# A masked attention block with residual norms: turned x kept twice by parity instead of copied, V's part of TensorE's loop written twice, and other ring sizes

## The reference

```python
qkv = (x @ w_qkv).reshape(b, n, 3, H, hd).transpose(2, 0, 3, 1, 4)
q, k, v = (qkv[0], qkv[1], qkv[2])
attn = jnp.einsum('bhnd,bhmd->bhnm', q, k) * scale
attn = jnp.where(attn_mask[None, None] == 0, -jnp.inf, attn)
attn = jax.nn.softmax(attn, axis=-1)
o = jnp.einsum('bhnm,bhmd->bhnd', attn, v).transpose(0, 2, 1, 3).reshape(b, n, d)
o = o @ w_proj + b_proj
...
return o + ln          # ln: layer norm of o with gamma and beta
...
x = _layernorm(x + _L0_gnn_ref(x, ...), axis=-1)
```

## Time and profile before

| | us |
|---|---|
| median of 3 runs | 3217.51 |
| lowest to highest | 3217.07 to 3221.09 |
| the profiled execution | 3214.41 |
| its span in the trace | 3212.6 |
| TensorE busy in it | 3035.8 |
| VectorE busy | 2481.6 |
| ScalarE busy | 2621.1 |
| GpSimd busy | 2500.2 |

### The profile page before, as it was taken

The page is one execution under the profiler, slowest core; times in us unless marked ns, Lnnn a source line. Parts: engine busy times, 40 slices in busy tenths (PEclk is TensorE's granted clock), DMA queues, the critical chain, the costliest instruction groups (busy, mean ns, idle before and its releaser), DMA issues.

```text
span 3212.6 us, 121377 instructions
## 1 busy us (share of the span) xinstructions
PE 3035.8 (94%) x42504; PEld 1892.9 (59%) x42504; DVE 2481.6 (77%) x4601; ACT 2621.1 (82%) x3849; POOL 2500.2 (78%) x1543
## 2 busy tenths in 40 slices
PE   6989999999999999999999999999999999999984
PEld 3656656656665656656566666656656566665552
DVE  5567777878778787787878878787787877878775
ACT  5888888888888888888888888888888888888871
POOL 2777878787887878888787887878878788887883
PEclk9999999999999999999999999999999999999997
DMA  7999999999999999999999999999999999999993
GB/s 208 192 190 199 208 198 211 199 211 205 206 212 197 214 202 206 213 199 211 200 210 205 207 211 197 215 201 206 214 199 208 199 210 206 207 212 187 202 197 97
DMA packets 2187078, 648.05 MB, mean 202 GB/s; under 512 B 2135408, under 2 KB 2135408, under 8 KB 2186992
## 3 DMA queue, kind: packets, MB, share of 16 engines
q1 hardware_dynamic: 2133808, 548.28, 93.1%
q10 hardware_dynamic: 53184, 98.59, 9.3%
HBM read 76.28 MB, written 33.55 MB: 34 GB/s over the span
## 4 chain that ended last, share of the span: by engine, by line
POOL 45%; issue 31%; PE 10%; SPq 7%; DMA 2%; DVE 2%; ACT 1%; POOLq 1%; DVEq 0%; ACTq 0%
POOL p_split L780 37%; SPq L309 7%; POOL x_res L796 4%; PE scores_a L411 3%; PE side L375 2%; DMA pt<-p_split 2%; POOL norm L804 2%; POOL norm L799 2%; PE side L357 2%; PE proj L392 1%; PE pv_bank L432 1%; PE pv_bank L434 1%; PE pv_bank L433 1%; POOL shift L807 1%; POOLq L779 1%
## 5 line engine op out<-in xcount | busy, mean ns | idle before, releaser
L780 POOL TENSOR_TENSOR p_split<-p,p_split 128x1024 f16<-128x1024 f32 x1024 | 2178.6, 2144 | 642.8 <-ACT p_split L517 641.1
L504 ACT ACTIVATE p<-p,row_min 128x1024 f32<-128x1024 f32 x1024 | 1170.7, 1144 | 279.0 <-DVE row_min L662 277.1
L517 ACT ACTIVATE p_split<-p 128x1024 f16<-128x1024 f32 x1024 | 1047.2, 1046 | 120.4 <-DMA pt<-p_split 119.9
L432 PE MATMUL pv_bank<-v_both,pt 128*128 128x64 f16 x8192 | 830.5, 193 | 39.2 <-DMA pt<-p_split 31.2
L662 DVE CUSTOM_DVE_ANT_0 p<-scores_a,mask_q 128x1024 f32<-128x1024 f32 x512 | 626.2, 1223 | 309.4 <-PE scores_b L411 259.9
L434 PE MATMUL pv_bank<-v_both,pt 128*128 128x64 f16 x8192 | 831.4, 194 | 0.0
L433 PE MATMUL pv_bank<-v_both,pt 128*128 128x64 f16 x8192 | 831.3, 194 | 0.0
L432 PEld LDWEIGHTS pv_bank<-v_both,pt 128*128 128x128 f16 x8192 | 741.0, 98 | 126.5 <-issue 62.1
L433 PEld LDWEIGHTS pv_bank<-v_both,pt 128*128 128x128 f16 x8192 | 730.6, 98 | 67.9 <-issue 1.6
L434 PEld LDWEIGHTS pv_bank<-v_both,pt 128*128 128x128 f16 x8192 | 731.4, 98 | 0.0
L375 PE MATMUL side<-xt,w_hi 128*128 128x512 f16 x2048 | 636.0, 382 | 7.8 <-DVE q_lo L641 7.2
(11 more groups left out here) (80 smaller groups left out, 4411.2 us busy)
## 6 DMA issues: line engine op xcount, KB each, us to landing
x_in<-in_x ACTq DMA_DIRECT2D x60, 512.0 KB, 5.3
x_res<-in_x ACTq DMA_DIRECT2D x120, 256.0 KB, 3.5
out<-x_res ACTq DMA_DIRECT2D x120, 256.0 KB, 3.3
pt<-p_split SPq DMA_TRANSPOSE x1024, 4.9
pt<-in_adj SPq DMA_DIRECT2D x8, 512.0 KB, 10.0
ot<-in_L_gnn_w_qkv SPq DMA_DIRECT2D x4, 768.0 KB, 9.7
p<-in_x SPq DMA_DIRECT2D x8, 256.0 KB, 5.0
p<-in_x ACTq DMA_DIRECT2D x8, 256.0 KB, 8.5
```

Source lines behind the costliest of these rows:

```text
L432: nc.tensor.matmul(o, hi, v_hi, start=(kt == 0 and at == 0), stop=False, skip_group_check=True)
L504: nc.scalar.activation(p32[:, slot, :], p32[:, slot, :], ACT.Exp, bias=row_min[:, slot:slot + 1], scale=-1.0, accum_out=row_sum[:, head:he ...
L517: nc.scalar.activation(p_split[:, head % RING, HI, :], p32[:, head % RING, :], ACT.Copy).then_inc(hi_done, 1)
L780: nc.gpsimd.tensor_tensor(p_split[:, slot, LO, :], p32[:, slot, :], p_split[:, slot, HI, :], ALU.subtract).then_inc(lo_done, 1)
```

## The change

- `xt` becomes two whole sets of 8 tiles, by the parity of the batch. X writes into the other set; there are no copies, no Ifs on VectorE and no waits for copies on TensorE. TensorE's wait for X1 moves from K1 to Q0.
- Q and K now have both operands at a register's address. For V, whose weights must stand at a fixed address, TensorE's loop body has slots 4 to 11 twice, each in an If on the parity of the batch. With it the scores, the products with V and the first projection matmul that lie in these slots stand twice. Outside the loop nothing is doubled.
- `p_split` becomes a ring of 8 heads, `pt` one of 4: ScalarE waits for the transpose eight heads back, SyncE for the product with V four heads back.
- Slots: `COST` of Q 8 to 9 and of X 8 to 5, the first projection run 3 to 4 matmuls, VectorE's takes of V0, V1, X1 from 12, 12, 18 to 10, 11, 15, the load of x from 20 to 18, one norm step from 36 to 34. VectorE's takes wait without the separate no-op.

```diff
-TURNED = 8
+TURNED = 4
+SPLIT = 8
...
-ORDER = [("Q1", 0, 12), ("X0", 0, 4), ("V0", 0, 48), ("V1", 0, 48), ("P0", 0, 3), ("O1", 0, 4), ("P0", 3, 7),
+ORDER = [("Q1", 0, 12), ("X0", 0, 4), ("V0", 0, 48), ("V1", 0, 48), ("P0", 0, 4), ("O1", 0, 4), ("P0", 4, 7),
...
-COST = {"Q": 8, "V": 2.5, "O": 4, "K": 10, "P": 9, "X": 8}
+COST = {"Q": 9, "V": 2.5, "O": 4, "K": 10, "P": 9, "X": 5}
...
+V_SLOTS = [s for s in range(SLOTS) if any(kind[0] == "V" for kind, i in ITEMS[s])]
...
-TAKE_DVE = {"Q1": 4, "X0": 5, "V0": 12, "V1": 12, "O1": 14, "X1": 18, "Q0": 22, "K0": 29, "K1": 30, "O0": 30}
-
-COPY = [12, 13, 13, 15, 16, 17, 17]
-LOAD_X = 20
+TAKE_DVE = {"Q1": 4, "X0": 5, "V0": 10, "V1": 11, "O1": 14, "X1": 15, "Q0": 22, "K0": 29, "K1": 30, "O0": 30}
+LOAD_X = 18
...
-              {"stats": 30, "aggr": 31, "eps": 33, "add": 34, "power": 35, "scale": 36, "sum": 38, "stats2": 38,
+              {"stats": 30, "aggr": 31, "eps": 33, "add": 34, "power": 35, "scale": 34, "sum": 38, "stats2": 38,
...
-        xt = sb("xt", [P, 2 * T - 1, 2, KC, P], F16)
+        xt = sb("xt", [P, 2, T, 2, KC, P], F16)
...
-        p_split = sb("p_split", [P, RING, 2, N], F16)
+        p_split = sb("p_split", [P, SPLIT, 2, N], F16)
...
-                    mm = nc.tensor.matmul(bank[:, c * P:(c + 1) * P], xt[:, place(t), rows, k, :],
+                    mm = nc.tensor.matmul(bank[:, c * P:(c + 1) * P], xt[:, side_of_x, t, rows, k, :],
                                           w[:, k, OF_V, pair(g), :],
...
-                    if i == 0 and kind == "K1" and active(g, "X1"):
+                    if i == 0 and kind == NEXT_FIRST and active(g, "X1"):
                         wait_alone(pe, side_dve, side_done(g, "X1"))
-                    if i == 0 and kind == NEXT_FIRST:
-                        wait_alone(pe, x_copied[0], batch(g + 1))
-                    if i == 0 and kind == "K1":
-                        wait_alone(pe, x_copied[1], batch(g + 1))
...
-                                          xt[:, place(4 * half):place(4 * half) + 4, x_half, k, :],
+                                          xt[:, parity(batch(of)), 4 * half:4 * half + 4, x_half, k, :],
...
+            def stretch(g, slots, side_of_x):
+                for s in slots:
+                    u, j = s // QUARTERS, s % QUARTERS
+                    if j == 0 and active(g, "A"):
+                        unit_scores(g, u)
+                    if j % 2:
+                        times_v(g, u, j // 2)
+                    for kind, i in ITEMS[s]:
+                        side_matmul(g, kind, i, side_of_x)
+
             def body(g):
...
+                if known(g):
+                    stretch(g, range(SLOTS), parity(batch(g)))
+                    return
+                stretch(g, range(0, V_SLOTS[0]), None)
+                for side_of_x in range(2):
+                    with pe.If((batch(g) & 1) == side_of_x):
+                        stretch(g, range(V_SLOTS[0], V_SLOTS[-1] + 1), side_of_x)
+                stretch(g, range(V_SLOTS[-1] + 1, SLOTS), None)
...
-                before = unit_before(ug, uk, RING // 2)
+                before = unit_before(ug, uk, SPLIT // 2)
...
-                wait_alone(dve, side_act, side_done(g, kind))
+                wait(dve, side_act, side_done(g, kind))
...
-            def copy_tile(g, t):
-
-                if t == 0:
-                    wait_alone(dve, side_ready, side_done(g, "V1"))
-                    wait_alone(dve, side_dve, side_done(g, "X0"))
-                move = nc.vector.tensor_copy(xt[:, place(t), :, :, :].rearrange("p h k n -> p (h k n)"),
-                                             xt[:, waiting(t // 2, t % 2), :, :, :].rearrange("p h k n -> p (h k n)"))
-                if t in (3, 6):
-                    move.then_inc(x_copied[t // 4], 1)
```

More of the change, by code:

```diff
@@ L236, in bodies @@
                 body(g)
[L238 to L251, removed]
         def heads(g, u, ab):
@@ L333, in first_turn, with side_matmul @@
                 mm.then_inc(x_first_turned, 1)
-            def side_matmul(g, kind, i):
+            def side_matmul(g, kind, i, side_of_x):
                 if not active(g, kind):
@@ L470, in first_high @@
                 act.wait_ge(x_first_turned, t + 1)
-                nc.scalar.activation(xt[:, place(t), HI, :, :], side[t % 2][:, :].rearrange("p (k n) -> p k n", k=KC), ACT.Copy
+                nc.scalar.activation(xt[:, 0, t, HI, :, :], side[t % 2][:, :].rearrange("p (k n) -> p k n", k=KC), ACT.Copy
                                      ).then_inc(x_first_hi, 1)
@@ L489, in take @@
                 elif kind[0] == "X":
-                    nc.scalar.activation(xt[:, waiting(g, half), HI, :, :],
+                    nc.scalar.activation(xt[:, parity(batch(g + PAIRS)), pair(g) * 2 + half, HI, :, :],
                                          bank[:, :].rearrange("p (k n) -> p k n", k=KC), ACT.Copy).then_inc(side_act, 1)
@@ L512, in high_part @@
                 head = 2 * uk + ab
-                before = unit_before(ug, uk, RING // 2)
+                before = unit_before(ug, uk, SPLIT // 2)
                 if not known(before[0]) or before[0] >= 0:
-                    wait(act, turned[(head - RING) % TURNED], turned_before(before[0], before[1], ab) + 16)
+                    wait(act, turned[(head - SPLIT) % TURNED], turned_before(before[0], before[1], ab) + 16)
                 act.wait_ge(exp_done, heads(ug, uk, ab) + 1)
-                nc.scalar.activation(p_split[:, head % RING, HI, :], p32[:, head % RING, :], ACT.Copy).then_inc(hi_done, 1)
+                nc.scalar.activation(p_split[:, head % SPLIT, HI, :], p32[:, head % RING, :], ACT.Copy).then_inc(hi_done, 1)
             def last_norm(g, i):
@@ L630, in take @@
                 elif kind[0] == "X":
-                    tile = waiting(g, half)
-                    nc.vector.tensor_tensor(xt[:, tile, LO, :, :], bank[:, :].rearrange("p (k n) -> p k n", k=KC),
-                                            xt[:, tile, HI, :, :], ALU.subtract).then_inc(side_dve, 1)
+                    at, tile = parity(batch(g + PAIRS)), pair(g) * 2 + half
+                    nc.vector.tensor_tensor(xt[:, at, tile, LO, :, :], bank[:, :].rearrange("p (k n) -> p k n", k=KC),
+                                            xt[:, at, tile, HI, :, :], ALU.subtract).then_inc(side_dve, 1)
                 elif kind[0] == "V":
@@ L743, in body @@
                                 take(bg, kind)
-                    for t in range(7):
-                        if COPY[t] == s:
-                            at_end(dve, g, lambda: copy_tile(g, t))
                     for i in range(2):
```

21 lines of the change are left out of this document (6 added, 15 removed).

## The result

The kernel after takes 3854.5 us (median of 4 runs, 3851.4 to 3861.3), the kernel before on the same chip 3217.3 (3216.5 to 3221.1): a ratio of 1.198, 95% interval 1.196 to 1.200. The forecast was 3447 with a range up to 3570, so the sign was right and the size was not: 637 us slower, where 230 were forecast.

What follows compares the result with a forecast made beforehand. TensorE was taken to bound three passes in four, VectorE's copies adding 4.9 us to the fourth. Sum: 3214.4 - 74 + 11 + 292 = 3443.4, as a median of runs 3447 us; range 3140 to 3570.

Steps and rivals of the forecast that it cites:

- two stalls a pass: TensorE's loop: the branch back and one If wait for absent blocks, 2.7 us each, +292 us; 42%.
- The rival of a loop that stays: TensorE's loop: no block is fetched inside it, so 3155 us, from 3135 to 3200; 35%.
- that of one stall: TensorE's loop: only the branch back waits, the Ifs land on present blocks; +146, 3301 us (3240 to 3350); 17%.
- The count behind it: TensorE's program: 1957 instructions a pass, 7.6 blocks, touch nine, ten with the one in advance; eight were seen to stay.
- straight running hides a fetch: TensorE's loop: a block reached without a branch arrives without a stall; only branches to a non-next block wait.
- some 5 where the clock falls with it: TensorE's instruction fetch: upper bound of a stall, some 5 us instead of 3.5, if the clock falls too.
- bound of 4.4 us for a stall: TensorE's two waiting branches a pass: the most a stall costs, 475 us in all over 54 passes.
- Copies gone: Batch ends: 15 passes lose 4.9 us each without VectorE's tile copies, -74 us.
- Registers, Ifs, slots and takes: TensorE's loop: two Ifs a pass +11 us (0 to 45); Q and K register addresses 0; slots and takes 0.
- they run ahead of matmuls of 512 columns: TensorE's Q and K: added register instructions are hidden by running ahead; taken 0, at most 55 us.
- Rings: Split ring of eight, turned ring of four: 0 us, transposes having 4 us to spare; binding rival 3187 alone, 2%.
- a stall up to 3.8 us: Upper end of the predicted range: two stalls a pass, each up to this size, giving 3570 us.

Runs made afterwards that it cites:

- 1960 instructions: The kernel after with only its TensorE loop's first instruction laid on the start of a block: 3799.5 us, 1.181 to the kernel before.
- the unaligned loop: The kernel after with only V's own matmuls twice, in six pieces (1789 instructions), the loop starting in mid-block: 3692.2 us, 1.148 to the kernel before.
- the hinted one: The kernel after with a prefetch hint for the branch back's target at the top of each TensorE pass: 3624.5 us, 1.126 to the kernel before.
- the whole loop without copies: The kernel before without the seven tile copies and their waits, later batches reading the first batch's x: 3137.4 us, 0.9755 to the kernel before.
- the old rings: The kernel after with the ring sizes of before (four split heads, eight turned): 3831.6 us, 1.191 to the kernel before.
- V by register: The kernel after with slots 4 to 11 once, V's weights also at a register's address (1545 instructions): 3252.5 us, 1.012 to the kernel before.
- V alone, aligned: The kernel after with only V's matmuls twice, in six pieces (1789 instructions), loop start on a block's start: 3255.3 us, 1.012 to the kernel before.
- the second stretch alone: The kernel before with only TensorE's slots 4 to 11 written twice in two Ifs, both with the same addresses: 3879.3 us, 1.207 to the kernel before.

## Why the prediction was wrong, by its own steps

**The case was the right one.** Of the prediction's cases, two stalls a pass (42%) came true: ten blocks a pass, two waiting branches, at the branch back and at an If. The rival of a loop that stays (35%, 3155) and that of one stall (17%, 3301) fell by the ten fetches and the two branches of the first profile. The count behind it, from packets and passes alone, held to the block in the loops of 1789 and 1960 instructions. Its "straight running hides a fetch" held in the kernel after, but not in the unaligned loop nor in the hinted one. The one-stall rival rested on a block replaced only by the one eight further on; the unaligned one of the pair has all nine fetched instead, which excludes it.

**The step that failed is "two stalls a pass, each 2.7 us"**, +292. It took the packet's 1.1 us, a load's 2.2 and a lead of 0.6. Measured are branches of 4.6 and 5.0 us. The packet's own time was right (0.9 to 1.1 us as a rule); the round about it was not: from the branch's start to the packet's 1.4 to 3.2 us, with a median of 2.3 at the branch back, and from the packet's end to the next instruction some 1.4. A load's time to land was the wrong row to be nearest to, since nothing says that a fetch is issued as promptly, or that the engine goes on when it lands. TensorE's waits in the kernel after, over the loop alone, have the two stalls in their first row:

```profile
PE scores_a L389 <- issue: 476.1, 106, 5.5
PE pv_bank L410 <- DMA pt<-p_split: 26.8, 48, 0.9
PE side L353 <- issue: 15.4, 26, 0.6
```

**That is 4.5 us a stall, 9.0 a pass and 476 us, where 2.7, 5.4 and 292 were forecast.**

**The clock was left out of the sum**, the second part of the same step. The upper bound had it ("some 5 where the clock falls with it"), as an end of the range and not a term. The two rows below are the whole loop without copies and in the kernel after:

```profile
326.10:2815.40 2489.30, 2470.69 (x35199) 1549.96 (x35196) 1940.55 (x3711) 2161.57 (x3185) 2063.70 (x1273) 1.00 1.06 212
```

```profile
326.80:3532.90 3206.10, 2679.38 (x35194) 1622.78 (x35191) 1946.94 (x3711) 2179.78 (x3180) 2057.64 (x1273) 0.92 0.99 167
```

For the same matmuls TensorE is busy **3.9 us a pass longer, 209 us in all**. The clock can account for all of it: 8.0 us of a pass's busy time lie at the lower level, where the score matmuls follow each other at twice the distance (0.43 us for 0.21), so that half of the 8.0, some 4.0 a pass, is the estimate of its cost. The stretches of the earlier trace rows show this very thing behind a wait of some 3 us, and the forecast's own stall was about as long. A stall that long should have carried it. With it the bound of 4.4 us for a stall, 475 in all, was too low: (476 + 209) / 106 = 6.5 each.

**Copies gone: right.** -74 forecast, -76 measured without them, -73 over 53 passes by the means 48.35 and 46.97.

**Registers, Ifs, slots and takes: about right.** +11 forecast for the Ifs and 0 for the rest. In the kernel after the clock leaves nothing over in TensorE's busy time, and its idle time without the two stalls is 0.96 us a pass against 0.35 without copies: 32 us more. In the fence of waits above stand 27 us of waits for transposes and 15 at the register addresses of Q and K, neither of which the loop without copies has; "they run ahead of matmuls of 512 columns" was wrong for one of these matmuls in every second pass. The loops that fetch nothing are slower than the copies' absence alone, by 2.13 us a pass (V by register) and 2.35 (V alone, aligned), but 1.1 and 0.8 of that are V's own matmuls, by edits that the kernel after doesn't have. Register addresses of Q and K are 0.3 to 0.5 more; what is left of the 2.13 and the 2.35 wasn't taken apart.

**Rings: right alone, wrong in company.** Some 23 us of the stalls' delay come through the shorter ring; with the old rings the loop's waits for transposes are 1.1 us instead of 26.8. They are inside the terms above.

Sum for the profiled span: 3212.6 - 73 + 476 + 209 + 32 = 3857, less 3 outside the loop 3854, against 3852.6. That this closes proves little, since the terms are differences between the same kernels' passes. What a separate kernel confirms is the cause: the second stretch alone, in the kernel before, has the stalls without the rest, and its passes are 12.3 us longer (60.67), 8.7 of it idle and 3.6 busy.

**The price of a stall isn't fixed.** Both together cost 12.3 us a pass (the second stretch alone against the kernel before). One at the branch back costs 8.1 (unaligned against aligned), with a wait along the straight in it. With the one at the branch back taken away by the hint, 4.4 came back, with such a wait put in its place. The one at the If was never alone against the same loop without it. Why a straight stretch waits for its block in two of the runs and not in the kernel after stays open.

**The range** reached to 3570 because its upper end was "a stall up to 3.8 us", drawn in from the bound. It should have gone to the bound: 3443 - 292 + 475 is 3626. Even that misses 3854 by some 230: the waiting alone measured 4.5 us a stall, more than the bound, and the clock came on top.

## What to carry to other kernels

Before a loop's body is written twice, count its instructions in blocks, with its real start and the block fetched in advance. A TensorE loop that touches eight blocks so counted costs nothing for code; one more block cost 8 us a pass here, more than the change could ever bring (4.9 us in every fourth pass). Where a body is a little too long, align its start, write twice only the instructions that need it, or use a register's address; the last two cost 0.8 and 1.1 us a pass here at V's short matmuls, and neither kernel beat the one before. And when an engine's idle time is charged, charge what the clock does after it too.

When a side engine's copies cost time, look whether their duration is their own: seven copies moved to slots where GpSimd was idle gave 70 of the 76 us that removing them would, with a line of slots and one wait.

## What the runs showed of the hardware that wasn't expected

- TensorE's taken branch to a block that isn't on the chip took 3.4 to 6.3 us (means of 4.6 back and 5.0 at the If), four to five times the packet's 1.06 us; one to a block that is there 0.21.
- Away from branches a block can come late too: waits of 1.2 us a pass in the unaligned loop and 1.3 in the hinted one, up to 2.2 and 2.1, none like them in the aligned loop of the unaligned one's instructions or in the kernel after.
- Eight blocks of 256 instructions stay, the one fetched ahead of need among them, and one block more means that all are fetched in every pass (0 or 9 fetches a pass for the same 1789 instructions, 3255 or 3692 us).
- A hint at the top of the pass, some 50 us ahead of the branch, cut it to 0.46 us in the median.
- The granted clock fell to 1.2 GHz for 3.4 or 6.8 us with 107 of 113 idle stretches of over 3 us (median 4.4); it cost 3.9 us a pass beside the 9.0 of waiting.
- A VectorE copy of 128x1024 float16 took 0.41 us in a gap of GpSimd's and up to 2.2 beside it.
- Register addresses ahead of V's matmuls cost 1.1 us of their busy time a pass (409.78 us for 352.06 over 53 passes).
